# An adaptive-norm attention and feed-forward block on one core: the gate's rows in a fourth column tile, fewer idle products, another stage order

## The reference

```python
mod = (_silu(L0_c) @ L0_wmod).reshape(L0_c.shape[0], 6, 1, -1)
sa, ca, ga, sb, cb, gb = (mod[:, i] for i in range(6))
ga = (2 * (ga >= 0) - 1) * jnp.maximum(jnp.abs(ga), 0.25)
gb = (2 * (gb >= 0) - 1) * jnp.maximum(jnp.abs(gb), 0.25)
h = _layernorm(x, axis=-1) * (1 + ca) + sa
x = x + ga * _L0_attn_ref(h, ...)    # conv of 3 taps to q, k, v (128 each); 16 heads of 64; causal blocks of 128
h = _layernorm(x, axis=-1) * (1 + cb) + sb
x = x + gb * _L0_ffn_ref(h, ...)     # base linear + top-2 of 16 experts of rank 64
```

## Time and profile before

| | |
|---|---|
| median of 3 runs | 461.55 us (459.86 to 462.46) |
| the profiled execution | 460.72 us |
| its span | 458.9 us |
| TensorE busy | 432.5 us, 94% of the span |
| DVE, ACT, POOL busy | 348.9, 300.7, 268.3 us |
| granted TensorE clock, mean | 0.988 of full speed |

### The profile page before, as it was taken

The page is one execution under the profiler, slowest core; times in us unless marked ns, Lnnn a source line. Parts: engine busy times, 40 slices in busy tenths (PEclk is TensorE's granted clock), DMA queues, the critical chain, the costliest instruction groups (busy, mean ns, idle before and its releaser), DMA issues.

```text
span 458.9 us, 11354 instructions
## 1 busy us (share of the span) xinstructions
PE 432.5 (94%) x4270; PEld 284.8 (62%) x4270; DVE 348.9 (76%) x683; ACT 300.7 (66%) x976; POOL 268.3 (58%) x313
## 2 busy tenths in 40 slices
PE   8899989999999989989999999988999999788996
PEld 8466558678787657654678666646676665344442
DVE  4697798988999978868678775668887988654851
ACT  1463778998897969866667866656778776721220
POOL 5021842451457986747667737463648778876681
PEclk9999989999999999999999999989999999999999
DMA  8995376752756497487572696518554472861542
GB/s 314 372 384 212 51 181 165 197 101 47 139 125 152 54 202 149 129 177 149 120 156 48 104 179 111 117 56 148 110 116 93 90 157 55 144 134 38 127 111 70
DMA packets 140678, 64.06 MB, mean 140 GB/s; under 512 B 130480, under 2 KB 130736, under 8 KB 140240
## 3 DMA queue, kind: packets, MB, share of 16 engines
q1 hardware_dynamic: 140480, 63.32, 60.0%
q10 hardware_dynamic: 144, 0.02, 0.0%
HBM read 26.63 MB, written 4.19 MB: 67 GB/s over the span
## 4 chain that ended last, share of the span: by engine, by line
PE 60%; DVE 15%; DMA 8%; POOL 7%; ACT 4%; SPq 3%; issue 2%; POOLq 0%; ACTq 0%
PE C L1175 15%; PE F L1047 15%; PE C L1047 11%; DMA gT<-g 5%; PE W L1238 4%; DVE cw L890 3%; PE W L1047 3%; PE S L1221 3%; PE S L1047 3%; PE F L1064 2%; DMA xb<-in_x_dram 2%; DVE g L1030 2%; ACT prob L724 2%; POOL prob L599 2%; PE S L1213 1%
## 5 line engine op out<-in xcount | busy, mean ns | idle before, releaser
L1175 PE MATMUL C<-hT,cw 128*128 128x256 f16 x864 | 109.2, 276 | 2.7 <-DVE cv L908 2.0
L599 POOL TENSOR_TENSOR prob<-prob,rinv 128x1024 f32<-128x1024 f32 x32 | 60.7, 1896 | 65.1 <-DVE rinv L942 65.0
L1175 PEld LDWEIGHTS C<-hT,cw 128*128 128x128 f16 x864 | 83.4, 99 | 21.5 <-issue 2.6
L724 ACT ACTIVATE prob<-S,nms 128x128 f32<-128x128 f32 x256 | 89.9, 377 | 4.1 <-DVE p L937 3.2
L1047 PE MATMUL F<-btw,gT 128*128 128x512 f16 x336 | 76.6, 385 | 6.0 <-DMA gT<-g 6.0
L695 ACT ACTIVATE qk<-C,bqk 128x256 f16<-128x256 f32 x128 | 52.7, 486 | 23.4 <-PE C L1047 22.9
L917 DVE SCALAR_TENSOR_TENSOR qk<-C,bqk,qk 128x256 f16<-128x256 f32 x128 | 54.5, 475 | 9.1 <-ACT qk L695 8.6
L1047 PEld LDWEIGHTS F<-btw,gT 128*128 128x128 f16 x336 | 32.6, 99 | 46.1 <-DMA gT<-g 7.4
L724 ACT ACTIVATION_READ_ACCUMULATOR prob<-S,nms 128x1 f32 x256 | 55.5, 217 | 0.0
L1047 PE MATMUL C<-cv,pw 128*128 128x256 f16 x384 | 51.6, 277 | 2.1 <-DVE xb L958 1.9
L937 DVE SCALAR_TENSOR_TENSOR p<-prob,p 128x1024 f16<-128x1024 f32 x32 | 45.7, 1427 | 3.6 <-ACT p L733 3.5
(11 more groups left out here) (198 smaller groups left out, 753.3 us busy)
## 6 DMA issues: line engine op xcount, KB each, us to landing
xa<-in_x_dram SPq DMA_DIRECT2D x10, 512.0 KB, 4.9
xb<-in_x_dram SPq DMA_DIRECT2D x6, 512.0 KB, 5.2
wmb<-in_wmod_dram SPq DMA_DIRECT2D x1, 3072.0 KB, 17.7
out_dram<-xb SPq DMA_DIRECT2D x12, 256.0 KB, 2.0
cw_raw<-in_cw_dram SPq DMA_DIRECT2D x3, 768.0 KB, 10.6
raw<-in_cw_dram SPq DMA_DIRECT2D x3, 768.0 KB, 5.3
wma<-in_wmod_dram SPq DMA_DIRECT2D x4, 512.0 KB, 6.8
bt_raw<-in_btw_dram SPq DMA_DIRECT2D x2, 1024.0 KB, 5.7
```

Of the source, the lines that this page charges most:

```text
L599: nc.gpsimd.tensor_tensor(prob[:], prob[:], rinv[:, i % 2].unsqueeze(2).broadcast_to([P, 8, P]), ALU.mult).then_inc(p_normal, 1)
L724: ins = nc.scalar.activation(prob[:, h], S[i % len(S)][h // 4][:, (h % 4) * P:(h % 4 + 1) * P], ACT.Exp, bias=nms[:, i % 2, h:h + 1], scal ...
L1175: ins = nc.tensor.matmul(bank_c[:, 0:CH], cw[:, i, a, c, tap, :], hT[:, j % 2, b, c, OWN - 1 + tap:OWN - 1 + tap + CH], start=step == 0, s ...
```

## The change

- `row:0:2`, `cols:0:2` and their copy and clamp are gone. `row:0:3` makes four rows in four strips: shift, scale, the attention's gate (from a buffer of its own, `ga_raw`) and the feed-forward's gate. It waits for both loads. `cols:0:1` turns four rows, one `clamp` works on both gates.
- `pick:0:0` and `pick:0:1` now follow `cols:0:1`, in the feed-forward's banks `F[0]` and `F[1]`; before they used the scores' banks. The first scores no longer wait for them.
- SP loads `wmb` right behind `ga_raw` and `wow_raw`; the first two residual blocks `xb` come last of that lot.
- 15 idle products stand where 32 stood.
- `SCHEDULE` is new from end to end; the work of each engine is otherwise the same.

```diff
-    N_CONST, N_IDENT, N_WARM = 12, 3, 32
+    N_CONST, N_IDENT, N_WARM = 12, 3, 15
...
-        na:0:0 sil:0:0 na:1:0 nb:0:0 rp:0:0 ht:0:0 hs:0:0 ht:0:1 hs:0:1 row:0:0 nb:1:0 cols:0:0 ht:1:0 ht:1:1 sp:0:0
+        na:0:0 sil:0:0 nb:0:0 na:1:0 rp:0:0 ht:0:0 hs:0:0 ht:0:1 hs:0:1 row:0:0 nb:1:0 cols:0:0 ht:1:0 ht:1:1 sp:0:0
...
                     if n > 0:
-                        pe.wait_ge(ld["ga" if n == 2 else "wmb"], 16)
+                        pe.wait_ge(ld["ga"], 16)
+                        pe.wait_ge(ld["wmb"], 16)
...
-                        for i, m in enumerate([(0, 1), (), (2,), (0, 1, 2)][n]):
-                            ins = nc.tensor.matmul(m_bank(("row", 0, n))[QUAD * i:QUAD * (i + 1), :], silw[:, k, :], held[:, k, m, :],
+                        for i, row in enumerate([wma[:, k, 0], wma[:, k, 1]] if n == 0 else
+                                                [wmb[:, k, 0], wmb[:, k, 1], ga_raw[:, k], wmb[:, k, 2]]):
+                            ins = nc.tensor.matmul(m_bank(("row", 0, n))[QUAD * i:QUAD * (i + 1), :], silw[:, k, :], row,
...
-                    rows = (2, 3, 1)[n]
+                    rows = (2, 4)[n]
...
-                        ins = clamp(gate[:, 2 - n], at[:, rows - 1, :, 0:NB])
+                        ins = clamp(gate[:], at[:, 2:4, :, 0:NB])
...
-                        pe.wait_ge(m_done, mod_by(("pick", 0), ("pick", 1)))
+
+                        pe.wait_ge(m_done, mod_by(("row", 0)))
+                        pe.wait_ge(t_lo, 3)
```

More of the change, by code:

```diff
@@ new lines, in bass_adaln_block @@
+        nb:2:0 c:0:9 e:0:0 c:0:3 nz:0:0 hs:2:0 cols:0:1 qk:0:3 s:0:1 m:0:1 ph:0:0 qk:0:2 v:0:3 pick:0:1 c:1:6
+        pick:0:0 halo:2:0 c:1:3 bias:0:0 pick:0:2 c:1:9 e:0:1 c:1:6 nz:0:1 c:1:6 s:0:2 pj:0:0 na:3:0 c:1:3 m:0:2
+        c:1:3 pick:0:3 ph:0:1 v:0:0 pk:0:0 qk:1:0 e:0:2 pj:0:1 c:1:24 nb:3:0 nz:0:2 c:1:12 pk:0:1 v:0:2 qk:1:1
+        pv:0:0 qk:1:5 ph:0:2 s:0:3 m:0:3 qk:1:4 v:0:1 c:1:12 sp:0:7 c:1:3 e:0:3 c:1:12 nz:0:3 c:1:9 hs:3:0 fbias:0:0
+        qk:1:3 qk:1:2 pv:0:1 v:1:0 ph:0:3 s:1:0 m:1:0 xr:0:0 v:1:2 v:1:1 halo:3:0 c:2:3 sp:0:9 e:1:0 c:2:3 nz:1:0
@@ L270, in bass_adaln_block @@
         everything = place[0]
-        cw_raw, pw_raw, ga_row = overlay(early, middle, ("cw_raw", [P, 3, DC, TAPS, P], F32),
-                                         ("pw_raw", [P, 3, HE], F32), ("ga_row", [QUAD, D], F32))
+        cw_raw, pw_raw = overlay(early, middle, ("cw_raw", [P, 3, DC, TAPS, P], F32),
+                                         ("pw_raw", [P, 3, HE], F32))
         pjw_raw, pjt = overlay(g_at, g_end, ("pjw_raw", [P, D], F32), ("pjt", [P, D], F32))
@@ L345, in bass_adaln_block @@
                    ffn_split(arw, raw_ar, 1, (ld["raw"], 96))]
-        M_BANK = {("row", 0, 0): S[0][0], ("cols", 0, 0): W[0], ("vb", 0, 1): F[1], ("pick", 0, 0): S[0][0],
-                  ("pick", 0, 1): S[0][1], ("bias", 0, 0): W[0]}
+        M_BANK = {("row", 0, 0): S[0][0], ("cols", 0, 0): W[0], ("vb", 0, 1): F[1], ("pick", 0, 1): F[1], ("bias", 0, 0): W[0]}
         w_bank = lambda stage: W[W_USE[stage] % len(W)]
@@ L433, in _ @@
                                  ).then_inc(ld["pb"], 16)
-                    for i in range(2):
-                        sp.dma_start(xb[:, i], xin[i]).then_inc(ld_xb[i], 16)
-                    sp.dma_start(wmb[:], wmod_v[:, :, 3:6, :]).then_inc(ld["wmb"], 16)
                     sp.dma_start(bb_row[:], bb_in.rearrange("(a d) -> a d", a=1).broadcast_to([QUAD, D])
@@ L439, in _ @@
                     sp.dma_start(ar_raw[:], ar_in).then_inc(ld["ar"], 16)
+                    for i in range(2):
+                        sp.dma_start(xb[:, i], xin[i]).then_inc(ld_xb[i], 16)
                 elif s == "hs" and j >= 2:
@@ L721, in _ @@
                     if j == 0 and n < 2:
-                        act.wait_ge(m_full, mod_by(("row", 0), ("row", 2)))
+                        act.wait_ge(m_full, mod_by(("row", 0)))
                     for h in range(8):
@@ L1080, in _ @@
                     if n > 0:
-                        pe.wait_ge(ld["ga" if n == 2 else "wmb"], 16)
+                        pe.wait_ge(ld["ga"], 16)
+                        pe.wait_ge(ld["wmb"], 16)
                     if n > 0 and m_before(stage):
                         pe.wait_ge(m_done, m_before(stage))
-                    held = wma if n < 3 else wmb
                     for k in (range(DC) if n > 0 else range(2) if s == "rp" else range(2, DC)):
@@ L1094, in _ @@
                     pe.wait_ge(pool_chain, N_IDENT)
-                    pe.wait_ge(m_done, max(mod_by(("row", (0, 3, 2)[n])), m_before(stage)))
-                    rows = (row_ab, row_cdg, ga_row)[n]
+                    pe.wait_ge(m_done, max(mod_by(("row", (0, 3)[n])), m_before(stage)))
+                    rows = (row_ab, row_cdg)[n]
                     r = rows.shape[0]
@@ L1135, in _ @@
                 elif s == "pick":
-                    of, b = (("cols", 2), ("cols", 1), ("fbias", 0))[n // 2], n % 2
+                    of, b = (("cols", 1), ("cols", 1), ("fbias", 0))[n // 2], n % 2
                     pe.wait_ge(m_done, max(mod_by(of), m_before(stage)))
```

98 lines of the change are left out of this document (46 added, 52 removed).

## The result

The changed kernel takes 483.73 us (median of 6 runs, 480.12 to 484.39) against 460.71 us (6 runs, 458.56 to 462.46) in the same comparison: ratio 1.048, 95% interval 1.044 to 1.052. It is slower by 23 us, where 454.0 us and a range of 448.5 to 459.5 were predicted. The profiled execution took 480.37 us, its span is 478.5 us.

What follows compares the result with a forecast made beforehand. TensorE, busy 432.5 of 458.9 us, was taken as the bound. 460.7 less 7.8 (4.0 work, 3.8 front idle) is 452.9; 0.8 to the median and 0.3 for DVE give 454.0 us, range 448.5 to 459.5.

Steps and rivals of the forecast that it cites:

- The fourth strip: In `row:0:3`: added strip costs nothing, 0.8 us at most; with `row:0:2` and `cols:0:2` gone, 4.0 us less TensorE work.
- The rival with a price for the strip: At `row:0:3`: the four products queue behind the other twelve, the 3.6 us come back, 457.6 us; chance 0.03.
- the rule quoted with it: Skill's note on TensorE column groups: quadrant 3's bus has a hardware bug and is not supported; by it 457.6 us.
- The front: From the start to the first scores: these start at about 33.5 us, before at 44.78; 3.8 us idle time gone.
- this rival: In the front: clock falls to 1.2 GHz for the `vb` products, up to 1.7 us more, 455 us; no separate chance.
- It is worth that much because TensorE has no idle time around these products: Around the removed row products: 4.0 us less work counts in full, as TensorE is busy 24.26 of 25 us.
- the sum 4.0 + 3.8: Whole kernel: 4.0 us of removed TensorE work plus 3.8 us of front idle time gone, 7.8 us gained.
- DVE gives it back: From 20 to 120 us: DVE, squeezed to 94%, hands waits on and the clock falls; 457 to 461 us, chance 0.17.
- I find no reason for a sum of either sign, and take 3 us as the spread each way: Stage order behind the front: no net gain or loss from the new list, spread 3 us each way.
- units of scores stand at 6 us or more from each other: Stage order behind the front: spacing of score units said to hold in both lists; no size of its own.
- Slower: At ten close places `gT` comes late, 12 to 20 us of waits against 7.8 gained; 465 us, chance 0.05.
- a sign of being wrong: In the changed profile: `gT` waits of TensorE over 10 us in sum, 6.0 us before.

Runs made afterwards that it cites:

- e1: Changed kernel's four strips, joint clamp, 15 idle products and load order, with the old stage list; 460.88 us, ratio 1.0006 to the kernel before.
- e2: Kernel before with 15 idle products for 32 and nothing else; 462.31 us, ratio 1.0033.
- e10: Kernel before with base and low-rank feed-forward products in one pass of three, 83 us less TensorE work; 447.21 us, ratio 0.974.
- e3: Changed kernel with one word, `sp:0:14`, moved behind `fb:3:0`; four executions of 472.87, 479.64, 482.08 and 482.43 us.
- e13: e11 with four `fl` moved later, behind the work that followed them; 484.75 us, ratio 1.051 to the kernel before.
- e14: e1 with the old list up to nz:6:1 (about 330 us) and the new one from there; 472.77 us, ratio 1.028 to the kernel before.
- e11: e1 with the new list from qk:6:5 on and `sp:0:14` moved behind `fb:3:0`; 475.05 us, ratio 1.030 to the kernel before.
- e15: e1 with the old list up to v:7:3 (about 400 us) and the new one from there; 468.43 us, ratio 1.018 to the kernel before.
- e12: Changed kernel with `sp:0:14` moved behind `fb:3:0` and the list of e1 from qk:6:5 on; 464.34 us, ratio 1.007 to the kernel before.
- e6: e1 with the new list between pv:1:3 and qk:6:5 (about 127 to 300 us); 472.0 us, ratio 1.027 to the kernel before.

## Why the prediction was wrong

- **The fourth strip, right.** The 16 products of `row:0:3` ran from 38.95 to 42.6 us, 3.6 us for four strips where the earlier trace rows has 3.63 for three. The rival with a price for the strip fell, and the trace does not agree with the rule quoted with it.
- **The front, right in kind.** `row:0:0` ended at 12.7 us (12.5 said), TensorE waited 1.89 us for `cw_raw` (1.8), there was no wait for `wmb` (landed at 36.3 us, 34 to 38 said). The first scores came at 36.09 us instead of 33.5, since the clock fell behind that wait (4.47 us of `vb` products instead of 2.78; this rival came true) and DVE's splits ran to 30 us instead of 27. The second unit's came at 45.04, 1 us past the range. (A slip in the reading: DVE's share from 20 to 120 us is 88%, not 89; nothing hangs on it.)
- **"It is worth that much because TensorE has no idle time around these products", and the sum 4.0 + 3.8: wrong.** e1 keeps both parts, the term of 7.8 us, and gains nothing (ratio 1.0006). e2 shows a front 3.4 us earlier given back by the end, e10 that TensorE's work is not the measure. I read 94% as the bound and priced each microsecond in full. The Trainium skill, Perfetto Trace Analysis, section Identifying the Most-Contended Engine, says that the busy share of products is not a good measure of how close a kernel is to the machine's limit; e10, with 83 us less work and 13.4 us less time, agrees, though what it shows is a chain of dependences more than that measure's own fault. The rival *DVE gives it back* named the right outcome for these parts (457 to 461; e1 took 460.88), and gave it 0.17; its mechanism is borne out in part, as e1 lost its lead behind a wait for `gT` and one for DVE's `cv`.
- **"I find no reason for a sum of either sign, and take 3 us as the spread each way": the step that failed.** This term, nothing with 3 us each way, measured 22.9 us (after 483.73 against e1 460.88): by the medians about 5 in the first third, nothing in the middle without the stall of `sp:0:14`, and some 14 in the last. The traces of the changed kernel and of e3 place 4.8 us at the stall, and 7 to 9 lie between s:6:1 and s:7:3 in every kernel with the new list there. I had compared how many `gT` readers stand close behind their producer, and that "units of scores stand at 6 us or more from each other", and nothing else: not which engine an in-order stage blocks, not what fills the waits. At s:7:1 the new list has 7 us to the next unit, within my rule, and waits there. Going through the list for stages that overwrite something a later stage reads would have shown `sp:0:14` ahead of `fb:3:0`.
- **The rival *Slower* had the right sign, 465 us, by late `gT`, and that is at best part of it.** `gT` waits rose from 6.0 to 10.6 us, past the 10 that the prediction had named as a sign of being wrong. e13 took most of them out of the last third and was 9.7 us slower.
- **Clock.** Products at 1.2 GHz behind waits are about 6 us of the 23 (7.8 us issued less, 1.6 us busy less), a term that I had only for the front.

Shown are that the list alone makes the loss (e1), that the stall goes with one word moved (e3), and that the stretch from s:6:1 to s:7:3 loses with the new list and not with the old (e14 and e11 against e15 and e12). That the thin place behind s:7:1 is half of what costs there is read from the timelines; no run moved `wo:6:0` alone. What the stall is worth by itself depends on what lies behind it: 4.8 us in e3, nothing by s:6:1 in e11. Open are the 5 us of the first third, and what else the last third's medians hold beyond that stretch. That e6 costs 11 us while e12's middle costs nothing is explained by the stall only in part; e6 also has a wait of 3.68 us for `h` at 136 us and a half clock behind it, next to its first splice.

## What to carry to other kernels

A busy share of 94% does not say that the engine's work is the bound. Before a microsecond of it is priced in full, take a large piece out (e10) and see what the time does. When a list of stages is rewritten, price each place by what fills each wait there and by which in-order engine a stage can block, not by counts of close pairs; the total work, the same in both lists, said nothing here. A reader moved away from its producer can take its cover away from another wait. And before a difference of medians is given to a place, lay the two traces side by side from the start: here kernels with one and the same list came to a stage 2 to 4 us apart.

## What was not expected of the hardware

DVE's tiny operations were slow beside POOL. The clamp on 128x16 elements, timeline of DVE and of POOL in the changed kernel:

```profile
45.78 1.66 DVE L799 SCALAR_TENSOR_TENSOR tmpcol<-gate 128x16 f32<-128x16 f32 x1
47.48 1.08 DVE L800 TENSOR_SCALAR silT<-gate 128x16 f32<-128x16 f32 x1
48.59 1.07 DVE L801 TENSOR_SCALAR tmpcol<-tmpcol 128x16 f32<-128x16 f32 x1
49.70 0.17 DVE L802 SCALAR_TENSOR_TENSOR gate<-silT,tmpcol 128x16 f32<-128x16 f32 x1
```

```profile
45.52 1.90 POOL L599 TENSOR_TENSOR prob<-prob,rinv 128x1024 f32<-128x1024 f32 x1 [4.66 <-DVE rinv L939]
47.37 2.27 POOL L564 TENSOR_TENSOR h<-xa,h 128x512 f16<-128x512 f32 x2
```

Three of these operations end within 0.03 us of the end of a POOL operation (47.41, then the two of 1.1 us each, at 48.53 and 49.64); the fourth, with POOL free, takes 0.17. In the kernel before they took 0.17 us each on half the columns, with POOL idle, and in e1, on the same 128x16 elements and with POOL idle, 0.17 to 0.18 each (50.93 to 51.74 us). So it is not the size. The gate is 3.3 us late by that, and TensorE waits 2.29 us for it with half the clock behind. The Trainium skill, SBUF — State Buffer, section Who interferes with whom, says that a DVE operation in a two-port mode and a GpSimd operation shut each other out for a whole instruction, and that one with two inputs in SBUF contends with a GpSimd operation that reads SBUF. These three rows agree; in which mode the DVE operations ran, the trace doesn't show. It was one of the costs of moving the clamp in time, and no row of the kernel before showed it.
